# A transformer-style image block with routed experts: the residual of the expert stage moved from VectorE to TensorE, and its write-out to ScalarE

## The reference, cut to what matters

```python
x = x + _L0_conv_ref(_ln_c(x), ...)          # windowed attention
t = _to_tokens(x)
t = t + _L0_ffn_ref(_ln_t(t), ...)           # top-2 of 8 experts
x = _from_tokens(t, x)

# inside _L0_ffn_ref
router_probs = softmax(x @ router_w + router_b)
top_p, top_i = top_k(router_probs, 2);  top_p = top_p / sum(top_p)
expert_out = einsum('bnd,edc->bnec', x, expert_w) + expert_b
return einsum('bnk,bnkc->bnc', top_p, gathered)
```

## Time and profile before

| | us |
|---|---|
| median of 3 runs | 486.56 |
| the three runs | 486.3 to 486.81 |
| the profiled execution | 487.85 |
| its span, first to last instruction | 486.2 |
| TensorE, busy in the span | 402.4 (83%) |
| VectorE | 390.1 (80%) |
| ScalarE | 242.5 (50%) |
| GpSimd | 104.6 (22%) |

### The profile page before, as it was taken

How to read it: one execution, slowest core, us unless ns; L and a number is a source line. 1 busy time by engine, 2 the same in 40 slices (tenths; PEclk the granted TensorE clock), 3 DMA queues, 4 the chain that set the end, 5 groups by cost and what they waited for, 6 DMA issues and landing times.

```text
span 486.2 us, 12843 instructions
## 1 busy us (share of the span) xinstructions
PE 402.4 (83%) x4872; PEld 208.5 (43%) x4882; DVE 390.1 (80%) x511; ACT 242.5 (50%) x409; POOL 104.6 (22%) x152
## 2 busy tenths in 40 slices
PE   3786789999999999999999988469688698666863
PEld 1232346666666666666666543124234233111210
DVE  0389578999999999999999875976897997997643
ACT  3653367767777676677767670615323512102110
POOL 6730001011101110110111010003224324524632
PEclk9999779999999999999999998969899989879888
DMA  8400000000000000000000001932164737727541
GB/s 306 184 0 1 2 1 3 1 1 0 0 0 0 0 0 0 0 0 0 0 0 0 3 1 28 205 82 50 38 151 128 167 80 179 187 58 202 140 129 43
DMA packets 10901, 28.80 MB, mean 59 GB/s; under 512 B 3200, under 2 KB 4736, under 8 KB 10496
## 3 DMA queue, kind: packets, MB, share of 16 engines
q1 hardware_dynamic: 8400, 20.46, 16.6%
q0 software_dynamic: 2048, 6.29, 4.3%
q10 hardware_dynamic: 432, 1.77, 0.9%
HBM read 5.96 MB, written 4.19 MB: 21 GB/s over the span
## 4 chain that ended last, share of the span: by engine, by line
PE 45%; DVE 27%; issue 11%; ACT 6%; SPq 5%; DMA 2%; DVEq 1%; POOL 1%; POOLq 0%; ACTq 0%
PE psum L459 7%; DVE neg_max L927 6%; PE psum L321 5%; PE psum L476 5%; PE psum L341 4%; SPq L206 4%; PE psum L446 4%; PE psum L430 4%; DVE window_work L930 3%; PE psum L600 3%; PE psum L484 3%; PE psum L592 3%; PE psum L570 3%; DVE o_tok L938 2%; DVE rstd L363 2%
## 5 line engine op out<-in xcount | busy, mean ns | idle before, releaser
L728 ACT ACTIVATE probs<-psum 128x512 f32<-128x512 f32 x128 | 74.4, 594 | 25.1 <-PE psum L459 24.4
L930 DVE TENSOR_TENSOR window_work<-psum,neg_max 128x1024 f32<-128x1024 f32 x64 | 78.4, 1225 | 7.2
L927 DVE TENSOR_REDUCE neg_max<-psum 128x16 f32<-128x1024 f32 x64 | 77.0, 1203 | 7.3 <-PE psum L446 7.2
L459 PE MATMUL psum<-weights_sb,window_work 128*128 128x128 f32 x512 | 82.1, 283 | 0.9 <-ACT probs L728 0.9
L254 POOL TENSOR_TENSOR o_norm<-o_tok,o_rden 128x128 f32<-128x128 f32 x64 | 24.6, 406 | 249.8 <-DVE o_rden L940 249.8
L459 PEld LDWEIGHTS psum<-weights_sb,window_work 128*128 128x128 f32 x512 | 58.3, 142 | 43.5 <-issue 25.7
L476 PE MATMUL psum<-probs,v_cols 128*32 128x64 f32 x2048 | 55.4, 226 | 0.3 <-DVE o_tok L938 0.3
L592 PE MATMUL psum<-gate_rows,gate_sel_sb 128*128 128x512 bf16 (+1 forms) x118 | 42.3, 407 | 12.8 <-DVE window_work L1075 5.3
L1075 DVE TENSOR_TENSOR window_work<-stage,psum 128x512 f32<-128x512 f32 x48 | 31.8, 676 | 16.3 <-PE psum L592 10.9
L476 PEld LDWEIGHTS psum<-probs,v_cols 128*32 128x32 f32 x2048 | 34.6, 109 | 23.7 <-issue 20.6
L712 ACT ACTIVATE stage<-k_sb,weights_sb 128x512 f32<-128x512 f32 x64 | 44.3, 723 | 0.0
(11 more groups left out here) (95 smaller groups left out, 615.5 us busy)
## 6 DMA issues: line engine op xcount, KB each, us to landing
stage<-x_win SPq DMA_DIRECT2D x112, 128.0 KB, 2.6
out<-out_sb POOLq DMA_DIRECT2D x16, 256.0 KB, 2.5
stage<-in_x SPq DMA_DIRECT2D x3, 1024.0 KB, 14.4
stage<-x_win POOLq DMA_DIRECT2D x16, 128.0 KB, 3.7
gate_rows<-gate_parts SPq DMA_DIRECT2D x48, 32.0 KB, 1.8
stage<-in_x SPq DMA_DIRECT2D x2, 512.0 KB, 6.2
weights_sb<-weights ACTq DMA_DIRECT2D x1, 875.5 KB, 10.3
gate_f<-gate_sel ACTq DMA_DIRECT2D x1, 512.0 KB, 13.5
```

The costliest lines, as they stand in the source:

```text
L459: last = nc.tensor.transpose(bank[TURN_BANKS[v % 2]][:, b * P:b * P + P], heads.rearrange("p h k -> p (h k)"), const["c_ident"][:, :])
L728: nc.scalar.activation(probs[:, w % 4, :], bank[TURN_BANKS[w % 2]][:, :], ACT.Exp).then_inc(exp_done, 1)
L927: nc.vector.tensor_reduce(m_t, t, AX.X, ALU.max, negate=True).then_inc(max_done, 1)
L930: nc.vector.tensor_tensor(shifted_unit[:, unit % 2, :, :, :], t, m_t.unsqueeze(3).to_broadcast([P, IMG, HEADS, TOK]), ALU.add).then_inc(sh ...
```

## The change

TensorE gets one more product for each chunk: behind the bias it multiplies the chunk's token tile by the 128 x 128 identity `c_ident` and accumulates it in the same bank. The bank then holds the full sum, and ScalarE writes it out with a copy. VectorE's `combine` is gone. `out_sb`, the banks and the semaphores are the same; `summed` is now raised by ScalarE (VectorE still gives it its starting value).

```diff
@@ bias(quad, j), TensorE
                 nc.tensor.matmul(bank[6 + j % 2][:, :], const["c_eb"][:, j, :],
                                  gate_f32[:, bass.ds(quad * CHUNK, CHUNK)],
                                  start=True, stop=False, skip_group_check=True)
+                nc.tensor.matmul(bank[6 + j % 2][:, :], const["c_ident"][:, :], tokens(quad * QUAD + j, None),
+                                 start=False, stop=False, skip_group_check=True)
@@ ScalarE
+            def combine(quad, j):
+
+                c = quad * QUAD + j
+                act.wait_ge(y_step, c * 2 + (2 + Y))
+                act.wait_ge(out_free, c + 1)
+                nc.scalar.activation(out_sb[:, j % 2, :].rearrange("p (y win x) -> p win y x", win=NW, y=WS),
+                                     bank[6 + j % 2][:, :].rearrange("p (win y x) -> p win y x", win=NW, y=WS),
+                                     ACT.Copy).then_inc(summed, 1)
+
             def mixture(quad, gate_next=False, norm_next=False):
                 for j in range(QUAD):
                     for i in range(2):
                         copy_gates(quad, j, i)
+                        if i == 0 and j >= 1:
+                            combine(quad, j - 1)
...
+                combine(quad, QUAD - 1)
@@ VectorE
-            def combine(quad, j):
...
-                        if k == IMG - 1 and j >= 1:
-                            combine(quad, j - 1)
-                combine(quad, QUAD - 1)
```

More of the change, by code:

```diff
@@ L1048, in gates @@
                 one.then_inc(gate_step, 1)
-            def combine(quad, j):
-                c = quad * QUAD + j
-                dve.wait_ge(y_step, c * 2 + (2 + Y))
-                dve.wait_ge(out_free, c + 1)
-                nc.vector.tensor_tensor(
-                    out_sb[:, j % 2, :].rearrange("p (y win x) -> p win y x", win=NW, y=WS),
-                    bank[6 + j % 2][:, :].rearrange("p (win y x) -> p win y x", win=NW, y=WS),
-                    act_all[:, bass.ds(c * CHUNK, CHUNK)].rearrange("p (win y x) -> p win y x", win=NW, y=WS),
-                    ALU.add).then_inc(summed, 1)
             def mixture(quad, gate_next=False, norm_next=False):
```

## The result

| | before | changed |
|---|---|---|
| median, us (20 runs each, side by side) | 486.46 | 489.15 |
| ratio, with its 95% interval | | 1.0067 (1.0044 to 1.009) |
| profiled execution, us | 487.85 | 489.14 |
| its span, us | 486.2 | 487.2 |
| its mean granted TensorE clock | 0.943 | 0.954 |

A forecast was written before the change was run, and what follows sets the result against it. Bounds: mostly TensorE in loop chunks 0 and 3, later SyncE's 32.3 us DMA run. 3.4 + 2.2 + 0.7 - 1.2 + 2.5 - 0.35 - 2.6 - 0.5 = +4.15 on 486.56 gave 490.7 us, range 489.5 to 492.

The forecast's parts named there:

- rival A: Chunk 2, loop quads: GpSimd's product and VectorE's L1040 don't collide, 2.5 us fall away, 488.2; chance 0.22.
- rival B: Quad 2: identity product delays k_sb, GpSimd still meets L1026, only the addition's 0.6 comes, 492.7; chance 0.10.
- 1 product in chunks 0, 3: Quads 0 and 1: TensorE is the path there, identity product costs 4 x 0.86 = 3.4 us; elsewhere hidden.
- 2 write-out ahead of the root: Loop quads' chunk 1: ScalarE's write-out delays table load and root, reciprocal later by a new 1.1 us, twice, +2.2.
- 3 boundary: Between quads 0 and 1: last write-out delays logits and q_sb copy, TensorE waits, +0.7 us.
- 4 addition gone in chunk 2: Chunk 2 of quads 0 and 1: VectorE's addition was on the path, its removal saves 1.2 us.
- 5 L1026 of quad 1 freed: Quad 1: GpSimd runs ahead of VectorE's L1026, so their collision goes away, -0.35 us.
- 5 collision at L1040: Chunk 2, loop quads: GpSimd's earlier product stretches VectorE's L1040, ending at 361.0, +1.25 us, twice, +2.5.
- 6 quad 2: Quad 2, chunk 1: GpSimd's store no longer waits for VectorE, L1026 ends earlier, -2.6 us before SyncE's run.
- Rival C: Loop quads: VectorE is the bound, product free, eight additions saved, -7.9 us, 478.7; chance 0.07.
- Rival D: Terms cancel: ScalarE's table load may start while the write-out waits (-2.2), and no L1040 collision; 486.0 to 486.9; chance 0.12.
- Those 32.3 us are the same wherever they start: From SyncE's last DMA run at 435.3 to its last landing at 467.6: length unchanged by the edit.

The follow-up runs named there:

- e1: Kernel before plus the identity product alone; VectorE copies the bank out where it added: 492.32 us, ratio to before 1.0128.
- e2: Changed kernel without the identity product, so ScalarE's write-out alone (output lacks the residual): 485.18 us, ratio to before 0.996.
- e3: Changed kernel with one edit: ScalarE writes chunk 0 out behind chunk 1's root and exponential, not ahead: 483.9 us, ratio to before 0.9902.
- e7: e3 plus ScalarE computing the next quad's logits ahead of the last chunk's write-out: 483.4 us, ratio to before 0.9924.
- e10: Kernel before with the change only in chunks 1 and 2 of the loop quads and in quad 2: 480.76 us, ratio 0.9882.
- e9: Unchanged kernel with a test appended: GpSimd product near a VectorE instruction, two SBUF inputs each; the first keeps its time, the second pays up to 0.51 or 1.10 us.
- e12: Unchanged kernel with a test appended: GpSimd store issue, every second one followed by a product, near VectorE's addition; 0.38 us ahead of the product it took 2.21 us.
- e4: Kernel before with the change in quads 2 and 3 only, loop quads as before: 484.33 us, ratio to before 0.9934.
- e6: Kernel before with the change in quad 2 only, quads 0, 1 and 3 as before: 483.23 us, ratio to before 0.9904.
- e8: Changed kernel profiled once more, nothing altered: 491.18 us, quad 2 to SyncE 16.49 us.
- e11: e10 plus TensorE products nobody reads, ahead of the reciprocal wait in loop quads and quad 2's first experts: 479.37 us, ratio to before 0.985.

## Why the prediction was nearly right

It said slower, 490.7; it was 489.15, a median 2.7 above before's where +4.15 was forecast. The forecast's own mechanism didn't come whole: the collision of rival A stayed away and the relief of quad 2 failed as in rival B, which together would give 490.2. Term by term, in stage time:

| term | forecast | measured | shown by |
|---|---|---|---|
| 1 product in chunks 0, 3 | +3.4 | +3.4 | changed; e1 (3.3) |
| 2 write-out ahead of the root | +2.2 | +2.0 (1.05 and 0.99) | changed; e2 and e3 for the cause |
| 3 boundary | +0.7 | +0.56 | changed; e7 (0.53) |
| 4 addition gone in chunk 2 | -1.2 | -1.2 (0.68 and 0.54) | changed; e10 |
| 5 L1026 of quad 1 freed | -0.35 | about 0 | only read |
| 5 collision at L1040 | +2.5 | 0 | profile after, e9, e12 |
| quad 1's last experts to quad 2 | 0 | -0.3 | only read |
| up to quad 2 | +7.25 | +4.51 | |
| 6 quad 2 | -2.6 | -0.64; -2.8 in e4 | e4, e6, e8 |
| SyncE's run and landing | 0 | -1.40 (again: -0.85) | only read |
| tail | -0.5 | +0.48 (again: -0.7) | only read |

**Parts 1 to 4** stand, each to 0.2 us. Two of their sums are slightly off as written: part 2's makes 345.53 and not 345.6, and part 3's, with the branch, +0.9 and not +0.7. L1026 of quad 1 was freed (0.70 in place of 2.06), but chunk 1 there is longer by 0.99 where that of quad 0 is longer by 1.05, so it was worth 0.06 and not 0.35. **Rival C** is out by e1: with room in TensorE's list its product would have cost nothing. **Rival D** is out too, since the table load began only 0.01 us behind the write-out's end. The page named with rival C (the Trainium skill, Perfetto Trace Analysis, section Optimizing Scalar/DVE Operations) says that moving work off a saturated VectorE may make sense. The trace doesn't agree for chunks 0 and 3, and does for the chunks that e10 picks.

**Part 5 is the step that failed.** It put L1040's end at 361.0, "+1.25 us, twice", from L1026's rows. The time of GpSimd's move was right (359.1 to 359.4 forecast, 359.32 in the trace), and so was the overlap, but L1054 took 0.68 and the product 1.57. I had read the earlier trace rows as a law of who is stretched (VectorE, even as the first). e12 shows what was particular in them: a store issue directly ahead of the product. In the changed kernel GpSimd had idled 2.36 us for k_sb, with no store ahead. The Trainium skill, SBUF — State Buffer, section Who interferes with whom, has the starter keep the port. e9 agrees down to 0.04 us of recorded start. The earlier trace rows and e12 differ from it by the records, since a product can hold VectorE off up to 0.38 us before it shows. I gave the rival with that rule 0.22; what GpSimd did in the microsecond before each of the rows would have turned the chances round.

**Part 6 was right for the edit, and rival B, at 0.10, for this kernel.** e4 has part 6's product, its L1026 and its 2.7 us. In the changed kernel the half clock lasts from stage time 93.4 to 100, where before has it from 89.8 to 93.2. The experts at 426.33 then take 1.94 us, k_sb is late, GpSimd meets L1040 (1.62), and 0.64 is left, the 0.6 of rival B. B put the delay of k_sb down to the identity product; e4 and e6 have that product and the relief, so it isn't that alone. I had counted on a better clock ("with less idling ahead 0.86 could come back"), and the rows tie the loss to a worse one. Why the stretch is longer here is open: e3 has it short and e7 long, with the same edit in quad 2 and 0.5 us between them in the loop.

**"Those 32.3 us are the same wherever they start"** holds only to about 1 us: from SyncE's start to the landing it takes 32.20, 31.41, 31.95 and 31.28 in before's four profiles, and 30.80 and 31.35 in the changed kernel's two. By the chains, 0.65 of the 1.40 is issuing (29.00 against 28.35 from the first to the last issue) and 0.75 the landing (3.18 against 2.43). In before the fourth of the 16 issues took 2.11 us, and 1.44, 1.87 and 1.45 in the three more profiles of its stage; in the kernels that change quad 2 none of the first 16 took over 1.2. What holds it up is open, as no run tried it.

In stage time +4.15 became +2.95: 2.5 less from the collision, 0.24 less up to quad 2 otherwise, 1.96 more in quad 2, 1.40 less in SyncE's run, 0.98 more in the tail. With all profiles of the two kernels it became +2.5, and the last two terms move with the profile. So the near hit is in good part luck: two misses of about 2 us, in parts 5 and 6, against each other.

## What to carry to other kernels

Moving work off the busiest engine pays only where that engine is last; price each copy of the operation by its place in the chain (here chunks 0 and 3 cost, and 1, 2 and quad 2 together gained), and make the change only where it gains: a ratio of 1.0067 to before became 0.9882. An instruction that is queued ahead of another on an in-order engine hands its own wait on, so put the one with slack behind (e3, one reordering: the reciprocal starts 1.23 us earlier in quad 0). When a stretch is measured, look at the granted clock in it before explaining a rest of 1 to 3 us.

## What the runs showed of the hardware

- A VectorE instruction with two SBUF inputs and a GpSimd product of two SBUF tiles take turns: first by 0.04 us (VectorE) or 0.03 us (GpSimd) is enough. The second pays up to 0.51 (GpSimd) or 1.10 us (VectorE). A GpSimd product directly behind a store issue wins from up to 0.38 us before its record, and at 0.56 us it no longer does; the issue alone, in nine cases, left VectorE at 0.68 or 0.69 (e12).
- TensorE idles for the reciprocal ahead of L341: 3.57 us in before, 3.96 in the changed kernel, 4.82 in e2, and each time half clock followed in quad 0 (stage time 18 to 21). In e6, e9 and e12, which run before's code there, it came at 15 to 22 with the same 3.57, and the loop took 1.0 us longer. With the identity product ahead it idles 2.71: no half clock there in e1 and e3, but in e7 and e10, at 18 to 21. In quad 1 of e4 none followed 3.57. So the idle time alone doesn't tell, and what else does is open. In e11, with 0.99 us of idling, there was none in either quad, and chunk 1 of quad 0 was 1.09 us shorter than in e10.
- The clock fell again near 90 in all kernels but e10 and e11, for about 3.4 or 6.8 us, and where ScalarE writes out in quad 2 the longer piece goes with some 2 to 3.5 us more up to SyncE's run. The seven products that nobody reads raised the mean clock of the execution from 0.956 to 0.965 (e10, e11).
- ScalarE's table load began 0.01 us behind the write-out's end and the root 0.02 behind the load: it is just 1.28 us long here.
- SyncE's first 16 issues of its last run took 11.46 to 12.31 us in before's four profiles and 10.34 to 11.28 in the kernels that change quad 2. The store's DMA at the end of quad 1 took 2.51 us in before and 3.70 in e1. Why is open in both.
